# Two first dst and two sums per block: the halves of a graph kernel's edge blocks added up apart

## The chip, the cores and the metric

One core of a Trainium2 chip runs the whole kernel in one launch. The metric is the device time of one execution in microseconds, the median of several runs. Four compute engines matter: TensorE (PE, whose weight loads the profile lists as PEld), VectorE (DVE), ScalarE (ACT) and GpSimd (POOL). SyncE (SP) issues DMAs.

## The reference

There are V = 12500 nodes with 64 features and E = 400000 edges, sorted by `dst`. `src` is uniform; `dst` is drawn as `12500 * uniform ** 2`, so the density of edges falls from the low nodes to the high ones.

```python
h = x @ W_lin + b_lin
agg1 = segment_sum(h[src], dst) / deg
h = tanh(agg1 @ W1_agg + h @ W1_root + b1)
agg2 = segment_sum(h[src], dst) / deg
x = layernorm(x + tanh(agg2 @ W2_agg + h @ W2_root + b2))
hn = x @ Wn.T + bn
w = ssp(edge_feats @ We1.T + be1)          # ssp = softplus - log 2, per edge
w = ssp(w @ We2.T + be2)
agg = segment_sum(hn[src] * w, dst)
x = layernorm(x + ssp(agg @ Wc.T + bc) @ Wp.T + bp)
```

So there are three sums of gathered rows over the edges: two of 16-feature rows (stages e1 and e2) and one of 64-feature rows, each multiplied by an edge's gate (stage e3).

## The kernel before, in words

The edges are cut into NB = 125 blocks of 3200, each laid out as 128 partitions of SLOTS = 25 slots: partition p holds edges 25p to 25p + 24 of its block. Slots 0 to 12 are half 0 and slots 13 to 24 are half 1 (`HALVES`). With this layout each half has edges from the whole block.

A block is added up by matmul. For a window of WIN = 128 nodes, VectorE builds a one-hot matrix per slot (`make_hot`: is this edge's dst the w-th node of the window?), and TensorE multiplies each slot's gathered rows by it, 25 matmuls into one PSUM tile `sums` (`add_up`, L717 and L974). VectorE then adds `sums` onto the accumulator `acc` at the window's first node (L805 and L1153). That is one visit. A block needs as many visits as windows that its dst span, counted from its own first dst. The setup block computes for each block its first and last dst, hence the number of visits, a running count of them (`visits`), and subtracts the block's first dst from `dst_f`. `windows` reads from `visits` the registers of a block: since, to, and for VectorE the first dst. The visits are a loop from since to to.

Stages e1 and e2 run `pick_phase`. 14 of a block's slots are gathered from a table in memory by GpSimd, one indirect DMA a slot (L645), into one of four buffers. The other 11 slots are picked on chip: ScalarE makes one-hot keys (L666, L670), TensorE multiplies them with the table (L699, 88 matmuls of 400 columns a block), in four groups of 3, 3, 3 and 2 slots, and VectorE reduces the result (`take`, L758). After the fourth take VectorE splits the picked rows into bf16 parts (`parts`). TensorE's order is: pick group 0 of the next block, add up this block, pick groups 1, 2 and 3 of the next. `pick` waits for ScalarE's keys and for the take of the group before the last. VectorE's order is: read the registers, build half 0's hot of the first window, take(3), parts, then in each visit build half 1, build half 0 of the following window (also when there is none), wait for TensorE, and add; then `block_used` (L806), which frees the gather buffer for GpSimd four blocks on, and the takes 0 to 2 of the next block.

Stage e3 runs `gate_phase` with two gather buffers, 23 gathered slots (L922) and 2 picked ones (L957, 28 matmuls a slot). An edge MLP computes the gates: `first_layer` (L940) and `second_layer` (L947) on TensorE, logs and exponentials on ScalarE, the rest on VectorE. VectorE's `add_up` waits for a block's gathers, multiplies them by the gates (L1128), computes `second_values` of the next block (L1082), builds half 0's hot (L1116), takes the picked slot and runs the visits. TensorE's order is pick, second layer, pick, first layer of the block after next, add up.

All orders are written out by hand; there is no planner. SP loads keys, indices and edge features ahead.

Of the kernel before, what the change touches and what calls it, by code (L numbers as in the profile page):

```python
# [21 lines left out]
P = 128  # L22
# [63 lines left out]
def gnn_kernel(nc, x, xw, src, src_sel, src_gate, dst_all, edge_t, W_linT, b_lin, W1_agg, W1_root, b1, W2_parts, W2_diag, WnT, bn, We1T, be1,  # L86
               We2T, be2, WcT, bc, WpT, bp, out):
    ctx = ExitStack()
    with ctx:
# [40 lines left out]
        base_diag = sb("base_diag", [NB, NB])  # L130
# [33 lines left out]
        ext_t = sb("ext_t", [NB, 2])  # L164
        ext_i = sb("ext_i", [NB, 1], I32)
        win_lo = sb("win_lo", [NB, 1])
        win_hi = sb("win_hi", [NB, 1])
        win_n = sb("win_n", [NB, 1])
        win_row = sb("win_row", [1, NB])
        visits = sb("visits", [1, 3 * NB], I32)  # L170
# [104 lines left out]
        dst_ext = tiles.enter_context(nc.sbuf_tensor("dst_ext", [P, 2, NB], F32))  # L275
# [22 lines left out]
        with nc.Block() as block:  # L298
# [86 lines left out]
            def _(pe):  # L385
# [26 lines left out]
                for k in range(2):  # L412
# [3 lines left out]
                pe.matmul(bank[5][0:1, 0:NB], win_n[:, :], upto[0:NB, 0:NB], start=True, stop=True)  # L416
                pe.matmul(bank[5][0:1, NB:2 * NB], win_n[:, :], ident[0:NB, 0:NB], start=True, stop=True)
                pe.matmul(bank[5][0:1, 2 * NB:3 * NB], win_lo[:, :], ident[0:NB, 0:NB], start=True, stop=True)
                pe.matmul(bank[7][:, 0:NB], ones_all[:, :], base_diag[:, :], start=True,
# [6 lines left out]
            def _(dve):  # L426
# [33 lines left out]
                for c in range(2):  # L460
                    if c == 1:
# [3 lines left out]
                        dve.tensor_reduce(dst_ext[:, 0, :], dst_f[:, :, :], AX.X, ALU.min)  # L465
                        dve.tensor_reduce(dst_ext[:, 1, :], dst_f[:, :, :], AX.X, ALU.max).then_inc(small, 1)
# [66 lines left out]
                dve.tensor_reduce(ext_t[:, 0:1], bank[5][0:NB, 0:P], AX.X, ALU.min)  # L533
                dve.tensor_reduce(ext_t[:, 1:2], bank[5][0:NB, P:2 * P], AX.X, ALU.max)
                dve.drain()
                dve.tensor_copy(win_lo[:, :], ext_t[:, 0:1])
                dve.tensor_tensor(win_hi[:, :], ext_t[:, 1:2], ext_t[:, 0:1], ALU.subtract)
                dve.drain()
                dve.tensor_copy(ext_i[:, :], win_hi[:, :])
                dve.tensor_scalar(base_diag[:, :], ident[0:NB, 0:NB], win_lo[:, :], None, ALU.mult)  # L540
# [7 lines left out]
                dve.tensor_tensor(dst_f[:, :, :], dst_f[:, :, :],  # L548
# [22 lines left out]
        def pick_phase(tag, table, full, buf, hots, tiles):  # L571
# [34 lines left out]
            with nc.Block() as block:  # L606
# [133 lines left out]
                def _(dve):  # L740
# [46 lines left out]
                    def body(n, g, u):  # L787
# [903 lines left out]
```

## Time and profile before

| | |
|---|---|
| Median of 3 runs | 8763.72 us (8760.71 to 8766.48) |
| Profiled execution, first to last instruction | 8760.1 us |
| PE / PEld busy | 7637.1 us (87%) / 6905.6 us (79%) |
| DVE busy | 5505.1 us (63%) |
| ACT busy | 5860.1 us (67%) |
| POOL busy | 6259.5 us (71%) |
| Mean granted TensorE clock | 0.951 of full speed |

For the profiled execution the profile gives the span alone; the median of the runs is 3.6 us above it. e1 runs from about 96 to 2424 us, e2 to 4827 us, e3 from about 4960 to 8702 us; between them are short stages over the nodes.

A line of the profile's groups reads: source line, engine, operation, output<-inputs, shapes, count, then busy time and mean of one in ns, then idle time of the engine just before them and what ended it. Register reads and semaphore instructions are not counted as busy; an idle time that they end is put down to "issue". The engine name with a q is that engine's sequencer.

### The profile page before, as it was taken

How to read it: one execution, taken by the hardware profiler on the slowest of the kernel's cores; microseconds unless marked ns; L12 is line 12 of the kernel's file. 1: busy time of each engine (PE TensorE's matmuls, PEld its weight loads, DVE VectorE, ACT ScalarE, POOL GpSimd, SP SyncE). 2: the span in 40 equal slices, each digit the busy share in tenths (PEclk: the TensorE clock that was granted, in tenths of full speed). 3: DMA queues.
4: the chain of work that ended last, by engine and by line, in shares of the span. 5: the costliest groups of instructions: out<-in, count | busy, mean ns of one | idle time of the engine just before them, and what ended most of it. 6: DMA issues, size and time to landing. Idle time of an engine off the chain costs nothing. (4 is left out here: it accounts for less than half of the span.)

```text
span 8760.1 us, 165117 instructions
## 1 busy us (share of the span) xinstructions
PE 7637.1 (87%) x51516; PEld 6905.6 (79%) x51517; DVE 5505.1 (63%) x7447; ACT 5860.1 (67%) x10176; POOL 6259.5 (71%) x6471
## 2 busy tenths in 40 slices
PE   7999999999989999999999777777777777888887
PEld 6999999888889999998888666666666666776775
DVE  5655656666645555556666666666666666777777
ACT  5777777666657777776666566666666666666665
POOL 5777777766557777777664477777777777777776
PEclk9999999999989999999999798988988889999999
DMA  2111112111111111111111222222222222222222
GB/s 75 35 34 35 35 34 35 31 30 28 25 40 34 35 34 35 34 34 31 31 30 23 75 56 59 55 57 57 55 58 56 55 59 55 55 59 56 55 56 59
DMA packets 341135, 392.62 MB, mean 45 GB/s; under 512 B 165119, under 2 KB 240563, under 8 KB 340564
## 3 DMA queue, kind: packets, MB, share of 16 engines
q0 software_dynamic: 204000, 151.96, 12.1%
q1 hardware_dynamic: 136750, 239.87, 8.1%
q8 instruction: 32, 0.52, 0.0%
q14 instruction: 31, 0.25, 0.0%
q10 hardware_dynamic: 322, 0.03, 0.0%
HBM read 375.47 MB, written 15.92 MB: 45 GB/s over the span
## 5 line engine op out<-in xcount | busy, mean ns | idle before, releaser
L699 PE MATMUL banks<-split_sb,e_low_hot 128*128 128x400 f32 x22000 | 4092.6, 346 | 45.6 <-DVE split_sb L752 45.6
L699 PEld LDWEIGHTS banks<-split_sb,e_low_hot 128*128 128x128 f32 x22000 | 4015.6, 189 | 74.1 <-DVE split_sb L752 46.1
L922 POOL DMA_INDIRECT big<-hn_table,src_i x2875 | 2857.0, 994 | 883.7 <-issue 870.7
L645 POOL DMA_INDIRECT big<-p_table,src_i x1750 | 1655.8, 946 | 695.2 <-issue 528.7
L758 DVE TENSOR_REDUCE picked<-banks 128x48 f32<-128x1200 f32 x1000 | 1300.1, 1300 | 1352.1 <-PE banks L699 1351.1
L670 ACT ACTIVATE e_low_hot<-e_key_off 128x1536 fp32r<-128x1536 f16 x1000 | 1381.1, 1381 | 1130.6 <-PE banks L699 1112.7
L645 POOL DMA_INDIRECT big<-h_table,src_i x1750 | 1674.9, 957 | 612.5 <-issue 529.6
L666 ACT ACTIVATE e_key_off<-e_key_in,node_off 128x384 f16<-128x384 f16 (+1 forms) x4000 | 2028.4, 577 | 125.5 <-DMA e_key_in<-sel_dram 41.4
L957 PE MATMUL banks<-hn_split,e_low_hot 128*128 128x448 f32 x7000 | 1500.1, 370 | 75.5 <-issue 70.1
L957 PEld LDWEIGHTS banks<-hn_split,e_low_hot 128*128 128x128 f32 x7000 | 1298.0, 188 | 217.1 <-issue 96.6
L781 DVE TENSOR_TENSOR hot<-e_dst_pair,banks 128x1536 bf16<-128x1536 bf16 (+1 forms) x934 | 931.1, 997 | 69.9 <-issue 0.6
L1006 ACT ACTIVATE e_wide<-e_wide 128x512 f32<-128x512 f32 x500 | 268.9, 538 | 1041.3 <-DVE e_wide L1082 1041.3
L940 PE MATMUL banks<-e_wide,we 128*128 128x512 f32 x1000 | 553.5, 715 | 441.9 <-DVE e_wide L1082 431.7
L1116 DVE SCALAR_TENSOR_TENSOR hot<-dst_f,win_base,banks 128x1664 f32<-128x1664 f32 (+1 forms) x467 | 872.6, 1894 | 64.7 <-issue 50.3
L974 PEld LDWEIGHTS banks<-hot,big 128*64 128x64 f32 x8550 | 512.1, 144 | 397.0 <-DVE hot L1116 330.2
L974 PE MATMUL banks<-hot,big 128*64 128x128 f32 x8550 | 595.0, 289 | 262.7 <-DVE hot L1116 231.4
L940 PEld LDWEIGHTS banks<-e_wide,we 128*128 128x128 f32 x1000 | 254.0, 266 | 697.9 <-DVE e_wide L1082 521.8
L1128 DVE SCALAR_TENSOR_TENSOR big<-e_wide,big 128x1600 f32<-128x1600 f32 x125 | 228.3, 1826 | 891.8 <-DMA big<-hn_table,src_i 889.1
L1035 ACT ACTIVATE e_low_hot<-e_key_in,node_off 128x128 fp32r<-128x128 f16 x1750 | 535.7, 387 | 178.0 <-PE banks L957 178.0
L1012 ACT ACTIVATE e_wide<-e_wide 128x512 f32<-128x512 f32 x1000 | 550.3, 550 | 68.1
L1010 ACT ACTIVATE e_wide<-e_wide 128x512 f32<-128x512 f32 x1000 | 550.4, 550 | 67.7
L717 PE MATMUL banks<-hot,big 128*64 128x128 bf16 x8550 | 376.0, 226 | 209.1 <-DVE acc L805 114.0
(216 smaller groups left out, 4491.7 us busy)
## 6 DMA issues: line engine op xcount, KB each, us to landing
e_wide<-in_edge_t SPq DMA_DIRECT2D x125, 832.0 KB
e_key_in<-sel_dram SPq DMA_DIRECT2D x250, 343.8 KB
big<-hn_table,src_i POOLq DMA_INDIRECT x2875
big<-p_table,src_i POOLq DMA_INDIRECT x1750
big<-h_table,src_i POOLq DMA_INDIRECT x1750
e_key_in<-gate_dram SPq DMA_DIRECT2D x125, 64.0 KB
src_i<-in_src SPq DMA_DIRECT2D x375, 12.5 KB, 1.7
e_key_in<-sel_dram SPq DMA_DIRECT2D x250, 8.2 KB
```

The source lines that it names most:

```text
L645: pool.indirect_dma_start(buf[u][:, j, 0:ROW0], None, table, bass.IndirectOffsetOnAxis(ap=src_i[u][:, j:j + 1], axis=0),).then_inc(gathere ...
L666: act.activation(off[:, h, :], key_in[u][:, es], ACT.Abs, bias=node_off[:, h:h + 1])
L670: act.activation(low_hot[gr][:, :, :], off, ACT.Relu, bias=1.0, scale=-1.0).then_inc(low_made, 1)
L699: last = pe.matmul(o, low_hot[gr][:, h, e], split_sb[:, part, h * HI1:(h + 1) * HI1, :], start=(h == 0 and part == 0), stop=(h == HI2 - 1 ...
L758: dve.tensor_reduce(picked[:, AT[gr]:AT[gr] + SIZE[gr], :], found, AX.X, ALU.max).then_inc(pick_taken, 1)
L781: dve.tensor_tensor(hots[h].rearrange("p j (w t) -> p j w t", t=2), dst_pair[:, a:b, :].unsqueeze(2).to_broadcast([P, b - a, WIN // 2, 2]) ...
L922: pool.indirect_dma_start(buf[u][:, j, 0:F], None, table, bass.IndirectOffsetOnAxis(ap=src_i[u][:, j:j + 1], axis=0),).then_inc(gathered[u ...
L940: pe.matmul(pZ[q][:, 0:w], we1_2[:, :], xT_e[u][:, cs], start=True, stop=True).then_inc(z1_psum, 1)
L957: last = pe.matmul(bank[c][:, 0:GHALF * F], low_hot[s][:, h, :], hn_split[:, part, h * GHIGH + c * GHALF:h * GHIGH + (c + 1) * GHALF, :], ...
L974: last = pe.matmul(sums[c:c + F, 0:WIN], buf[u][:, j, 0:F], hots[h][:, j - a, :], start=(j < 2), stop=(j >= SLOTS - 2))
L1010: act.activation(o, o, ACT.Exp, scale=-1.0)
L1116: dve.scalar_tensor_tensor(hots[h], d.unsqueeze(2).to_broadcast([P, b - a, WIN]), win_base[:, bass.ds(window, 1)], iota_ps.unsqueeze(1).to ...
```

## The change

The host lays the edges out anew: the first 1664 edges of a block go to half 0 (partition p holds 13p to 13p + 12), the other 1536 to half 1 (12 a partition). `src`, `dst` and the edge features follow. Each half now has its own first dst, its own number of visits and running count, its own sums (columns 0 to 127 and 128 to 255 of a PSUM bank) and its own semaphore `acc_added`. A half's visits are a loop of their own on TensorE and on VectorE. No hot is built ahead of its visit.

```diff
-        def windows(eng, n, with_first):
-            since = eng.value_load(visits[0:1, bass.ds(n, 1)], ...)
-            to = eng.value_load(visits[0:1, bass.ds(n + NB, 1)], ...)
+        def windows(eng, n, h, with_first):
+            since = eng.value_load(visits[0:1, bass.ds(n + h * NB, 1)], ...)
+            to = eng.value_load(visits[0:1, bass.ds(n + (2 + h) * NB, 1)], ...)
             if not with_first:
                 return since, to, None
-            first = eng.value_load(visits[0:1, bass.ds(n + 2 * NB, 1)], ...)
+            first = eng.value_load(visits[0:1, bass.ds(n + (4 + h) * NB, 1)], ...)
...
             # pick_phase, TensorE
-                    def add_up(n, g, u):
-                        since, to, _ = windows(pe, n, False)
-                        pe.wait_ge(gathered[u], 16 * took * (g + 1))
-                        pe.wait_ge(msgs_made, n + 1)
+                    def add_up(h, n, g, u):
+                        a, b = HALVES[h]
+                        since, to, _ = windows(pe, n, h, False)
+                        if h == 0:
+                            pe.wait_ge(gathered[u], 16 * took * (g + 1))
+                        else:
+                            pe.wait_ge(msgs_made, n + 1)
                         pe.sem_inc(waited, 1)
                         with pe.Fori(since, to) as visit:
-                            pe.wait_ge(acc_added, visit + 1)
-                            for h, (a, b) in enumerate(HALVES):
-                                pe.wait_ge(hot_made[h], visit + 1 + (n if h == 0 else 0))
-                                for j in range(a, b):
-                                    ...
-                                last.then_inc(hot_used[h], 1)
+                            pe.wait_ge(acc_added[h], visit + 1)
+                            pe.wait_ge(hot_made[h], visit + 1)
+                            for j in range(a, b):
+                                ...
+                            last.then_inc(hot_used[h], 1)
                     def body(n, g, u):
                         if inside(n + 1):
                             pick(0, n + 1)
-                        add_up(n, g, u)
+                        add_up(0, n, g, u)
                         if inside(n + 1):
                             pick(1, n + 1)
+                        add_up(1, n, g, u)
+                        if inside(n + 1):
                             pick(2, n + 1)
                             pick(3, n + 1)
...
             # pick_phase, VectorE
-                    def body(n, g, u):
-                        since, to, first = windows(dve, n, True)
-                        make_hot(0, n, 0, since + 1)
-                        take(3, n)
-                        parts(u)
+                    def half(h, n, since, to, first):
                         with dve.Fori(since, to) as visit:
                             ...
-                            make_hot(1, n, window, visit + 1)
-                            make_hot(0, n, window + 1, visit + 2)
-                            dve.wait_ge(hot_used[1], visit + 2)
-                            dve.wait_ge(acc_added, visit + 1)
+                            make_hot(h, n, window, visit + 1)
+                            dve.wait_ge(hot_used[h], visit + 2)
                             a_w = acc[:, bass.ds(start, WIN)]
-                            dve.tensor_tensor(a_w, a_w, sums[:, 0:WIN], ALU.add).then_inc(acc_added, 1)
+                            dve.tensor_tensor(a_w, a_w, sums[h], ALU.add).then_inc(acc_added[h], 1)
+                    def body(n, g, u):
+                        since, to, first = windows(dve, n, 0, True)
+                        take(3, n)
+                        parts(u)
+                        half(0, n, since, to, first)
+                        if inside(n + 1):
+                            take(0, n + 1)
+                        since, to, first = windows(dve, n, 1, True)
+                        half(1, n, since, to, first)
                         dve.sem_inc(block_used, 1)
                         if inside(n + 1):
-                            for gr in range(3):
-                                take(gr, n + 1)
+                            take(1, n + 1)
+                            take(2, n + 1)
...
             # gate_phase, TensorE (add_up changed as above; its drain and block_used after half 1)
                     def body(n, g, u):
                         pick(n + 1, 0)
                         second_layer(n + 1)
                         pick(n + 1, 1)
+                        add_up(0, n, u)
                         if not isinstance(n, int) or n + 2 < NB:
                             first_layer(n + 2, turn_of(g, u) + 1, u % 2)
-                        add_up(n, g, u)
+                        add_up(1, n, u)
...
             # gate_phase, VectorE (half as above)
-                        make_hot(0, n, 0, since + 1)
+                        half(0, n, since, to, first)
                         if values_ahead:
                             take(n + 1, 1, (u + 1) % 2)
-                        with dve.Fori(since, to) as visit:
-                            ...
+                        since, to, first = windows(dve, n, 1, True)
+                        half(1, n, since, to, first)
...
             # host
+    def by_slot(a):
+        blocks = np.asarray(a).reshape(NB, EB, -1)
+        parts = [blocks[:, P * j:P * k].reshape(NB, P, k - j, -1) for j, k in HALVES]
+        return np.concatenate(parts, axis=2)
```

In the setup block the minima and maxima of dst are taken for each half (four reductions over halves instead of two over all slots), four rows are transposed instead of two, six row matmuls instead of three give the counts and first dst, the matmul with `base_diag` is twice as wide, `dst_f` is lowered in two subtractions, and `visits` is filled by four copies and two subtractions instead of two and one.

## Rows read from the trace of the kernel before

**Rows 1.** Windows by stretch: engines' busy us (instructions), then clock, DMA share, GB/s.

```profile
100.00:1458.00 1358.00, 1347.39 (x8822) 1308.11 (x8822) 803.86 (x1167) 1064.56 (x1561) 1027.01 (x1087) 1.00 0.19 35
1520.00:2424.00 904.00, 815.37 (x6029) 778.26 (x6028) 564.36 (x879) 580.53 (x851) 564.95 (x598) 0.98 0.15 28
...
5000.00:7320.00 2320.00, 1807.15 (x10976) 1449.60 (x10976) 1451.75 (x1724) 1460.81 (x3130) 1774.46 (x1790) 0.90 0.23 57
```

**Rows 2.** block_used by stretch: count, ns min/median/max, first to last start.

```profile
L806 DVEq EVENT_SEMAPHORE  x78: 21/21/21, 121.1 to 1458.8; - x78
L806 DVEq EVENT_SEMAPHORE  x44: 21/21/21, 1536.9 to 2424.1; - x44
L806 DVEq EVENT_SEMAPHORE  x78: 21/21/21, 2524.5 to 3864.8; - x78
L806 DVEq EVENT_SEMAPHORE  x45: 21/21/21, 3926.0 to 4827.1; - x45
```

**Rows 3.** The page's group of hot builds in e1 and e2: count, busy, mean.

```profile
L781 DVE TENSOR_TENSOR hot<-e_dst_pair,banks 128x1536 bf16<-128x1536 bf16 (+1 forms) x934 | 931.1, 997 | 69.9 <-issue 0.6
```

**Rows 4.** GpSimd's gathers, single-visit stretches of e1 and e2, columns of rows 2.

```profile
L645 POOL DMA_INDIRECT big<-p_table,src_i x1120: 940/944/1114, 149.9 to 1549.4; - x187
L645 POOL DMA_INDIRECT big<-h_table,src_i x1071: 951/955/1123, 2549.8 to 3899.7; - x179
```

**Rows 5.** Timeline, e1, one single-visit block: start, duration, engine, [idle before].

```profile
1006.45 16.27 PE L699 MATMUL banks<-split_sb,e_low_hot 128*128 128x400 f32 x88
1015.47 1.41 DVE L758 TENSOR_REDUCE picked<-banks 128x48 f32<-128x1200 f32 x1 [2.96 <-PE banks L699]
1018.26 0.24 DVE L778 TENSOR_SCALAR e_dst_pair<-dst_f,win_base 128x26 bf16 x1 [1.39 <-issue]
1019.52 0.98 DVE L758 TENSOR_REDUCE picked<-banks 128x32 f32<-128x800 f32 x1
1022.59 0.95 DVE L781 TENSOR_TENSOR hot<-e_dst_pair,banks 128x1536 bf16<-128x1536 bf16 x1
1022.64 0.42 PEld L717 LDWEIGHTS banks<-hot,big 128*64 128x64 bf16 x13 [0.27 <-issue]
1023.60 0.53 PE L717 MATMUL banks<-hot,big 128*64 128x128 bf16 x12 [0.38 <-DVE hot L781]
```

**Rows 6.** L717 single-visit, then two-visit: idle before, PE plus weight load, us, times.

```profile
  DVE hot L781: 27.5, 76
...
  DVE hot L781: 133.3, 170
  DVE acc L805: 53.7, 44
```

**Rows 7.** Timeline: the last block of e1, nothing queued before it.

```profile
2418.94 1.74 PE L717 MATMUL banks<-hot,big 128*64 128x128 bf16 x25 [3.46 <-issue]
```

**Rows 8.** e3's gating, single-visit then two-visit stretch, with its idle time.

```profile
L1128 DVE SCALAR_TENSOR_TENSOR big<-e_wide,big x76: 1824/1826/1827, 5045.2 to 7281.8; 128x1600 f32<-128x1600 f32 x76
  DMA big<-hn_table,src_i: 674.5, 76
...
L1128 DVE SCALAR_TENSOR_TENSOR big<-e_wide,big x45: 1824/1826/1827, 7341.5 to 8658.9; 128x1600 f32<-128x1600 f32 x45
  DMA big<-hn_table,src_i: 194.5, 45
```

**Rows 9.** Timeline, e3, one single-visit block.

```profile
5999.26 1.83 DVE L1128 SCALAR_TENSOR_TENSOR big<-e_wide,big 128x1600 f32<-128x1600 f32 x1 [9.06 <-DMA big<-hn_table,src_i]
6000.31 1.60 POOL L922 DMA_INDIRECT big<-hn_table,src_i  x1 [0.30 <-issue]
6011.63 0.29 DVE L1153 TENSOR_TENSOR acc<-acc,banks 128x128 f32 x1
```

**Rows 10.** Timeline of the setup block.

```profile
73.15 0.27 DVE L551 COPY win_row<-banks 1x125 f32<-1x125 f32 x1
```

More of the change, by code:

```diff
@@ L591, in pick_phase @@
             msgs_made = sem(f"{tag}_msgs_made")
-            sums = bank[7]
+            sums = [bank[7][:, h * WIN:(h + 1) * WIN] for h in range(2)]
             iota_ps = bank[6][:, 0:WIN // 2]
@@ L794, in body @@
                                 visit - since, 0, NW - 1,
-                                skip_runtime_bounds_check_because="a block's dst span NW windows at most")
+                                skip_runtime_bounds_check_because="a half's dst span NW windows at most")
                             start = nc.s_assert_within(
@@ L838, in gate_phase @@
             hot_used = [sem(f"{tag}_hot_used{h}") for h in range(2)]
-            acc_added = sem(f"{tag}_acc_added")
-            sums = bank[7]
+            acc_added = [sem(f"{tag}_acc_added{h}") for h in range(2)]
+            sums = [bank[7][:, h * WIN:(h + 1) * WIN] for h in range(2)]
             iota_ps = bank[6][:, 0:WIN]
@@ L1120, in make_hot, with half @@
                             ALU.subtract, ALU.is_equal).then_inc(hot_made[h], 1)
+                    def half(h, n, since, to, first):
+                        with dve.Fori(since, to) as visit:
+                            window = nc.s_assert_within(
+                                visit - since, 0, NW - 1,
+                                skip_runtime_bounds_check_because="a half's dst span NW windows at most")
+                            start = nc.s_assert_within(
+                                first + window * WIN, 0, V - 1,
+                                skip_runtime_bounds_check_because="a visit starts at or before a dst")
+                            make_hot(h, n, window, visit + 1)
+                            dve.wait_ge(hot_used[h], visit + 2)
+                            a_w = acc[:, bass.ds(start, WIN)]
+                            dve.tensor_tensor(a_w, a_w, sums[h], ALU.add).then_inc(acc_added[h], 1)
                     def add_up(n, g, u, values_ahead=True):
-                        since, to, first = windows(dve, n, True)
+                        since, to, first = windows(dve, n, 0, True)
                         dve.wait_ge(gathered[u], 16 * took * (g + 1))
@@ L1136, in add_up @@
                         dve.drain()
-                        make_hot(0, n, 0, since + 1)
+                        half(0, n, since, to, first)
                         if values_ahead:
                             take(n + 1, 1, (u + 1) % 2)
-                        with dve.Fori(since, to) as visit:
-                            window = nc.s_assert_within(
-                                visit - since, 0, NW - 1,
-                                skip_runtime_bounds_check_because="a block's dst span NW windows at most")
-                            start = nc.s_assert_within(
-                                first + window * WIN, 0, V - 1,
-                                skip_runtime_bounds_check_because="a visit starts at or before a dst")
-                            make_hot(1, n, window, visit + 1)
-                            make_hot(0, n, window + 1, visit + 2)
-                            dve.wait_ge(hot_used[1], visit + 2)
-                            dve.wait_ge(acc_added, visit + 1)
-                            a_w = acc[:, bass.ds(start, WIN)]
-                            dve.tensor_tensor(a_w, a_w, sums[:, 0:WIN], ALU.add).then_inc(acc_added, 1)
+                        since, to, first = windows(dve, n, 1, True)
+                        half(1, n, since, to, first)
                     def body(n, g, u):
```

122 lines of the change are left out of this document (69 added, 53 removed).

## The prediction

> **What bounds the kernel now.** I read the busy shares by stretch first [rows 1]. The run has three long stages, e1, e2 and e3. In e1's first stretch TensorE is busy 1347 of 1358 us at clock 1.00; GpSimd has 1027 us of gathers in the same time, and its gaps are short ones between gathers. So TensorE is at its limit there, with GpSimd close by. In e1's second stretch TensorE's share falls to 90% (815 of 904). In e3 it is 78% at clock 0.90: TensorE isn't the limit there.
>
> Then the signal with which VectorE ends a block [rows 2]. In e1's first stretch 77 intervals take 1458.8 - 121.1 us: 17.37 us a block. In the second it is (2424.1 - 1536.9) / 43 = 20.63, and in e2's second (4827.1 - 3926.0) / 44 = 20.48. The reference explains the step: dst is 12500 u^2, sorted, so block n of 125 spans about 0.8 (2n + 1) nodes. That is under 128 up to n = 79 and at most 199 after it: one visit, then two. The 934 hot builds of the two stages [rows 3] bear it out: each stage makes one for every block and two for every visit, 467 = 125 + 2 x 171. So there are 171 visits a stage, and 46 blocks have two.
>
> GpSimd sets a floor under both [rows 4]: 1399.5 us over 1119 gathers is 1.251 each, 14 a block, 17.51 us; in e2 (3899.7 - 2549.8) / 1070 makes 17.66.
>
> For e3 I read the gating operation, which starts when a block's gathers land [rows 8]. It recurs every (7281.8 - 5045.2) / 75 = 29.82 us with one visit and every 29.94 us with two, and VectorE sits idle for the gathers before every one of them: 8.9 us a block, then 4.3. One gather more or less is what e3 feels; a visit isn't.
>
> **Part 1: fewer visits in e1 and e2.** A half spans about half of a block's nodes: 0.8 (2n + 1) x 0.52, at most 104, so every half has one visit. Add-up matmuls fall from 171 x 25 to 125 x 25 a stage, hot builds from 467 to 250, and the two-visit blocks go. What one block costs afterwards I work out on the single-visit block of the timeline [rows 5]. From the first pick matmul (1006.45) to the add-up (1022.64) is 16.19 us for 88 matmuls, 0.183 each with one entry into an add-up; the entry shows 0.27 idle, 0.09 more than the usual spacing. The add-up itself is 0.55 for 13 (1022.64 to 1023.60 less the 0.38 wait is 0.58) and 0.52 for 12.
>
> **Part 2: the second entry.** TensorE now loads its two registers twice a block. Behind 24 queued pick matmuls that costs again 0.1 us net; with nothing queued it shows 3.46 us of idle time [rows 7], which is the upper bound. I take 0.1, since pick group 1 has as many matmuls as group 0.
>
> **Part 3: hot builds no longer made ahead.** Before, half 0's build ran before VectorE's take of group 3, and the next window's build was made whether wanted or not. Now half 0 is built after take(3) and the split into parts. TensorE's pick(0) starts 24 x 0.183 + 0.09 before 1022.64, at 1018.16, and the result of group 3 reaches VectorE at about 1018.4. Take(3) to the end of a build is 1019.52 to 1023.54 in the rows, 4.02; with 13 slots 4.1. So hot 0 is ready at 1022.5, 0.1 us before TensorE wants it: no wait, without slack. VectorE then waits for the add-up (1023.4), adds (0.28), takes group 0 (1.41), and reads three registers for half 1. The rows give that read: take dispatched 1015.47, next operation 1018.26, 2.8 us, of which 1.4 lies under the take. Starting the take at 1023.95, the build starts at 1026.7 and ends at 1027.95. TensorE, with pick(1) from 1023.2, is ready at 1027.7. That is a wait of 0.3 us. Behind it are picks 2 and 3; their takes have over 1 us to spare.
>
> One block: 16.19 + 0.55 + 0.52 + 0.1 + 0.3 = 17.65 us. Bounds: 17.35 without the wait, which GpSimd's 17.51 and 17.66 then replace; upward, an unhidden 3.46 twice a block is the far end, but the near rows are the waits for hot builds and sums in two-visit blocks [rows 6]: 133.3 + 53.7 us over 44 blocks, double counted for TensorE and its weight load, so some 2 us for four half add-ups, 0.5 each. With 0.5 at both halves it is 18.35.
>
> **Sum of e1 and e2.** From first to last signal is 2303.0 us in e1 and 2302.6 in e2 [rows 2]; after, 124 x 17.65 = 2188.6. The first signal comes later, 10.6 us instead of 6.1 us after its picks, +4.5. So -109.9 and -109.5: -219.
>
> **Part 4: e3.** Block 78's successors lose 0.12 us each: 45 x 0.12 = -5. The tail has one visit less: -2. The chain from gating to the last sum is now 12.7 us in a single-visit block (5999.26 to 6011.92) [rows 9]; after, the speculative build (about 1.9) goes, but there are two round trips to TensorE, two sums and a second register read: 16 to 18 us. That takes 4 to 5 of the 8.9 us idle, and about nothing where it is 4.3, as two visits go there. GpSimd waits for block_used two blocks back and has over 10 us left. ScalarE's first logs follow first_layer, which moves behind add_up(0): its first result comes about 2 us later, when ScalarE is just done with the second logs. Cover gone, each us of chain beyond the idle time costs 125 us.
>
> GpSimd's gather under the gating operation takes 1.60 us instead of 0.95 [rows 9], while e1's and e2's gathers, with hot builds beside them all the time, have a median within 4 ns of their shortest [rows 4]. So 217 hot builds fewer give GpSimd nothing in e3; the operation that it contends with stays.
>
> **Part 5: setup.** Two transposes, three row matmuls, four small copies and a subtraction more, and one more diagonal, each like the 0.27 of the win_row copy [rows 10], mostly in series: +2.5 us (0 to 5).
>
> **Sum.** 8760.1 - 219 - 7 + 2.5 = 8536.6 for the profiled execution; the runs' median lies 3.6 us above its span. Forecast 8540.
>
> **A rule weighed.** The rows have the three-register read at 2.8 us from the take's dispatch, and TensorE's exposed part at 0.27 us [rows 5]. The Trainium skill, DMA: Bandwidth & Descriptors (the table with the `tensor_load` floor), puts one such load at about 600 ns or more. By that figure alone TensorE's two loads are 1.2 us at each entry, and exposed they would make this change worth, by an estimate from that page, 250 x 1.1 = 275 us less than forecast, a loss. The trace disagrees for the exposed part behind a full queue, and agrees for VectorE, roughly.
>
> **Rivals.**
> A. No waits: hots arrive in time, and the floor is GpSimd. e1 at 17.5, e2 at 17.55 (its gathers start ahead of TensorE by two blocks): 248 x 0.12 = 30 us less, 8510. For it: TensorE's single-visit rate of 17.37 still holds waits. Against: half 1's chain on VectorE is 0.3 late by my own count.
> B. VectorE's chain becomes the bound. Each build, sum and register read is in series with TensorE, 0.6 us a block more: 248 x 0.6 = 149, 8690. For it: no slack at hot 0, and 20.6 us in two-visit blocks where VectorE and TensorE alternate. Against: there the second visit has no pick between, here each add-up has one.
> C. Slower: the register loads at the added entry are not hidden. From 0.9 us more a block (219 / 248) the gain is gone; at the rows' idle 3.46 less 0.27, every other block, it is 1.6 x 248 = 397, less 225: 8940. For it [rows 7]; against it [rows 5], with 24 matmuls ahead of the entry as now.
> D. Slower: e3 becomes chain-bound. Its clock is 0.90 on average already [rows 1], TensorE works in bursts after VectorE, and now in more of them; if the period passes 31.6 us (29.8 + 219 / 125) the gain is gone; at 32 it is 8540 + 270 = 8810. The Trainium skill, TensorE: Matmul & The Clock Gate (Part 1), says that activity releases the clock and idleness halves it. Against: the idle time of 8.9 us has to be used up first.
> E. The edit does not lower the visits (first dst per half far from the half's range): the numbers of dst above exclude it but for chance.
>
> **How the numbers follow.** Forecast 8540 (17.5 to 17.9 a block: 8510 to 8605) 0.58; A 0.17; B 0.17; C 0.03; D 0.04; E 0.01. What can be told from no change is 0.2%, 18 us. A, the forecast and nearly all of B are faster by more: 0.92. C, D and a B that goes further give slower 0.06; same 0.02. Range 8490 to 8650: the forecast's own, A, and B's nearer half.
>
> **What would show it.** L717 matmuls 6250, L781 500, L1116 250. Every block of e1 and e2 in 17.5 to 17.8 us, with no step at block 79. TensorE waits for hot builds at the second half, none at the first. The gating operation of e3 still every 29.8 us, with idle time before it of 4 to 5 us in all blocks. Wrong if a block of e1 takes over 18, if "issue" before L717 grows over 0.5 us each, or if that idle time in e3 is gone.

## The result and the profile after

The changed kernel takes 8527.36 us (median of four runs, 8525.02 to 8529.87) against 8764.24: a ratio of 0.9727, 95% interval 0.9713 to 0.9741. Run again beside the last experiments it took 8531.62 against 8762.99, 0.9736 (0.972 to 0.9752). The forecast was 8540, the range 8490 to 8650.

One thing has to be known to read the experiments: eight of the twelve (the first two runs of the old layout, and everything from "Both halves behind one pick group" to "e3: first_layer ahead; registers up front") ran while the kernel before itself took 12488 to 12524 us (medians), so their times stand only against one another, and what they say of the undisturbed kernel comes from the last blocks of a stage, which show no disturbance; the other four ran beside 8761 to 8763 us. None of the eight came out at the time, or in its loops at the time of a block, that was expected of it.

The page of the changed kernel has, in its first part, busy us (share of the span) and instructions, and in its fifth the groups (count, busy, mean ns, idle before):

```profile
PE 7506.0 (88%) x46924; PEld 6812.9 (80%) x46925; DVE 4727.1 (55%) x6607; ACT 5879.0 (69%) x10176; POOL 6267.9 (74%) x6471
...
L991 PE MATMUL banks<-hot,big 128*64 128x128 f32 x6250 | 563.3, 342 | 768.6 <-DVE hot L1137 768.6
L1137 DVE SCALAR_TENSOR_TENSOR hot<-dst_f,win_base,banks 128x1664 f32<-128x1664 f32 x250 | 470.3, 1881 | 270.2 <-issue 270.2
L794 DVE TENSOR_TENSOR hot<-e_dst_pair,banks 128x1664 bf16<-128x1664 bf16 x500 | 494.1, 988 | 44.4 <-issue 11.8
```

Hot builds in e1 and e2 are 500 in place of 934 [rows 3], and 250 in e3. The signal that ends a block, e1 then e2 (count, ns, first to last us), answers to [rows 2]:

```profile
L823 DVEq EVENT_SEMAPHORE  x125: 21/21/21, 129.1 to 2303.1; - x125
L823 DVEq EVENT_SEMAPHORE  x125: 21/21/21, 2409.1 to 4580.8; - x125
```

That is 2174.0 / 124 = 17.53 us a block and 2171.7 / 124 = 17.51, all the way through; the step at block 79 is gone. Windows in the middle of e1, e2 and e3 (columns of [rows 1]):

```profile
1000.00:2000.00 1000.00, 996.77 (x6455) 952.36 (x6454) 547.40 (x798) 777.87 (x1141) 756.81 (x799) 1.00 0.19 34
3500.00:4500.00 1000.00, 996.27 (x6450) 953.07 (x6449) 549.63 (x799) 778.52 (x1143) 758.58 (x793) 1.00 0.19 34
5500.00:7500.00 2000.00, 1559.40 (x9379) 1313.24 (x9380) 1133.35 (x1471) 1259.95 (x2676) 1531.19 (x1539) 0.89 0.23 56
```

TensorE is busy 99.7% of the time in e1 and e2, 90% before in e1's two-visit stretch. In e3 it is busy as before, at clock 0.89.

Where the 233.0 us between the two profiled spans (8760.1 and 8527.1) went, from the signals and the gatings of both traces: up to e1's first signal +8.1; e1 -129.0; from there to e2's first signal +5.6; e2 -130.9; to e3's first gating +1.3; e3 (first to last gating, 3688.3 and 3697.2) +8.9; tail +3.1.

One block of e1, cut to the two entries of the add-up (timeline; start, duration, engine, [idle before]); it answers to [rows 5]:

```profile
1507.46 1.02 DVE L794 TENSOR_TENSOR hot<-e_dst_pair,banks 128x1664 bf16<-128x1664 bf16 x1
1508.64 0.58 PE L728 MATMUL banks<-hot,big 128*64 128x128 bf16 x13
1509.15 4.64 PE L710 MATMUL banks<-split_sb,e_low_hot 128*128 128x400 f32 x24
1509.44 0.29 DVE L812 TENSOR_TENSOR acc<-acc,banks 128x128 f32 x1 [0.96 <-PE banks L728]
1509.72 1.41 DVE L771 TENSOR_REDUCE picked<-banks 128x48 f32<-128x1200 f32 x1
1512.42 0.24 DVE L791 TENSOR_SCALAR e_dst_pair<-dst_f,win_base 128x24 bf16 x1 [1.29 <-issue]
1512.73 0.95 DVE L794 TENSOR_TENSOR hot<-e_dst_pair,banks 128x1536 bf16<-128x1536 bf16 x1
1513.80 0.39 PEld L728 LDWEIGHTS banks<-hot,big 128*64 128x64 bf16 x12 [0.35 <-issue]
```

Hot 1 is built at 1513.69; TensorE's pick group 1 ends at 1513.79. The profile names no wait for a hot here. Over 1000 to 2000 us TensorE's weight load has 115 entries with idle time, all put down to "issue":

```profile
  issue: 36.8, 115
```

That is 0.32 us each, against 0.26 in the kernel before, where half 0's hot was ready 3.0 to 3.5 us early. There is a wait in it. TensorE's sequencer waits for the build's semaphore in one instruction of its own, at L725; in this block it is

```profile
L725 PEldq EVENT_SEMAPHORE  x1: 51/51/51, 1513.7 to 1513.7; - x1
```

and in the trace it starts 0.039 us after the build ends. It does so, to 0.001 us, in all 456 entries from 200 to 2200 and from 2500 to 4500 us, while the time since the last pick matmul varies: TensorE's sequencer is released by VectorE's build every time. At half 1 the weight load follows 0.115 us after the build's end in every block, with a mean idle time of 0.34 us in e1 and 0.36 in e2; at half 0 it is 0.30 and 0.26. So hot 1 comes about 0.1 us late in every block, and hot 0 at most 0.05.

In e3 the gating operation (count, ns, first and last us; then its idle time by cause) answers to [rows 8], and the timeline of one block to [rows 9]:

```profile
L1163 DVE SCALAR_TENSOR_TENSOR big<-e_wide,big x125: 1824/1826/1879, 4755.4 to 8452.6; 128x1600 f32<-128x1600 f32 x125
...
  DMA big<-hn_table,src_i: 285.0, 102
  issue: 31.6, 23
```

```profile
6004.09 1.82 DVE L1163 SCALAR_TENSOR_TENSOR big<-e_wide,big 128x1600 f32<-128x1600 f32 x1 [1.75 <-DMA big<-hn_table,src_i]
6014.33 1.08 DVE L1129 TENSOR_REDUCE big<-e_masked 128x64 f32<-128x896 f32 x1
6017.12 1.82 DVE L1137 SCALAR_TENSOR_TENSOR hot<-dst_f,win_base,banks 128x1536 f32<-128x1536 f32 x1 [1.70 <-issue]
6019.08 1.53 PE L991 MATMUL banks<-hot,big 128*64 128x128 f32 x24 [3.62 <-DVE hot L1137]
6020.83 0.29 DVE L1155 TENSOR_TENSOR acc<-acc,banks 128x128 f32 x1 [1.90 <-PE banks L991]
```

The period is still 3697.2 / 124 = 29.82 us. The chain from gating to last sum has become 6021.12 - 6004.09 = 17.0 us (12.7 before), and the idle time before a gating 316.6 / 125 = 2.5 us (8.9 and 4.3 before). At e3's start GpSimd now waits for its first buffer (0.6 us there before):

```profile
4773.74 1.01 POOL L940 DMA_INDIRECT big<-hn_table,src_i  x1 [5.63 <-PEq L995]
```

### The profile page after: what moved, and what is told of

Same layout as the page of the kernel before. It is cut to its first block and busy times, and to the rows that moved or that the text cites. A ratio compares the mean times of both kernels' runs of the same rounds, so it can differ in the third digit from the quotient of the medians.

```text
span 8527.1 us, 164066 instructions
## 1 busy us (share of the span) xinstructions
PE 7506.0 (88%) x46924; PEld 6812.9 (80%) x46925; DVE 4727.1 (55%) x6607; ACT 5879.0 (69%) x10176; POOL 6267.9 (74%) x6471
## 5 line engine op out<-in xcount | busy, mean ns | idle before, releaser
L710 PE MATMUL banks<-split_sb,e_low_hot 128*128 128x400 f32 x22000 | 4136.2, 346 | 46.8 <-DVE split_sb L765 25.2
L940 POOL DMA_INDIRECT big<-hn_table,src_i x2875 | 2860.6, 995 | 890.0 <-issue 859.0
L975 PE MATMUL banks<-hn_split,e_low_hot 128*128 128x448 f32 x7000 | 1594.5, 387 | 76.3 <-issue 69.8
L975 PEld LDWEIGHTS banks<-hn_split,e_low_hot 128*128 128x128 f32 x7000 | 1387.5, 201 | 236.0 <-issue 108.5
L991 PE MATMUL banks<-hot,big 128*64 128x128 f32 x6250 | 563.3, 342 | 768.6 <-DVE hot L1137 768.6
L1137 DVE SCALAR_TENSOR_TENSOR hot<-dst_f,win_base,banks 128x1664 f32<-128x1664 f32 x250 | 470.3, 1881 | 270.2 <-issue 270.2
L794 DVE TENSOR_TENSOR hot<-e_dst_pair,banks 128x1664 bf16<-128x1664 bf16 x500 | 494.1, 988 | 44.4 <-issue 11.8
L1126 DVE TENSOR_TENSOR e_masked<-banks,e_high 128x896 f32<-128x896 f32 x250 | 272.9, 1092 | 346.9 <-PE banks L975 326.3
L958 PE MATMUL banks<-e_wide,we 128*128 128x512 f32 x1000 | 426.8, 573 | 11.1 <-DMA e_wide<-in_edge_t 11.1
L1155 DVE TENSOR_TENSOR acc<-acc,banks 128x128 f32 x250 | 72.2, 289 | 656.3 <-PE banks L991 656.3
L1163 DVE SCALAR_TENSOR_TENSOR big<-e_wide,big 128x1600 f32<-128x1600 f32 x125 | 228.3, 1827 | 316.6 <-DMA big<-hn_table,src_i 285.0
```

What stands on the lines that cost most here:

```text
L710: last = pe.matmul(o, low_hot[gr][:, h, e], split_sb[:, part, h * HI1:(h + 1) * HI1, :], start=(h == 0 and part == 0), stop=(h == HI2 - 1 ...
L794: dve.tensor_tensor(hots[h].rearrange("p j (w t) -> p j w t", t=2), dst_pair[:, a:b, :].unsqueeze(2).to_broadcast([P, b - a, WIN // 2, 2]) ...
L940: pool.indirect_dma_start(buf[u][:, j, 0:F], None, table, bass.IndirectOffsetOnAxis(ap=src_i[u][:, j:j + 1], axis=0),).then_inc(gathered[u ...
L975: last = pe.matmul(bank[c][:, 0:GHALF * F], low_hot[s][:, h, :], hn_split[:, part, h * GHIGH + c * GHALF:h * GHIGH + (c + 1) * GHALF, :], ...
L991: last = pe.matmul(sums[h][c:c + F, :], buf[u][:, j, 0:F], hots[h][:, j - a, :], start=(j < a + 2), stop=(j >= b - 2))
```

## The experiments

The theory: the gain is the visits that the layout saves; the second entry costs TensorE next to nothing, because a pick group stands between the halves, and VectorE reaches hot 1 just in time; e3 stays bound by GpSimd. Rivals: the splitting of the sums alone gives the gain; VectorE or TensorE has reserve; e3's chain is about to take over.

### Old layout

```
-        blocks = np.asarray(a).reshape(NB, EB, -1)
-        parts = [blocks[:, P * j:P * k].reshape(NB, P, k - j, -1) for j, k in HALVES]
-        return np.concatenate(parts, axis=2)
+        return np.asarray(a).reshape(NB, P, SLOTS, -1)
```

> The changed kernel's program with the edges laid out as before: each half has edges of the whole block, so blocks from 79 on have two visits in each half. Theory 1 (the gain is the second visits that fall away; the new order by itself costs a little): the first 79 blocks of e1 keep 17.53 us, the later ones have two extra round trips between VectorE and TensorE of some 2.3 us each behind no pick work, 22 us or more, against 20.6 before; in e3 the chain of two-visit blocks grows by some 5 us and passes the 2.5 us of idle time that is left. Slower than before, 8850 to 9050 us. Rival (the gain is the order: no hot built ahead, sums apart behind two pick groups): the time stays under 8650 us, and the later blocks of e1 take at most 19 us.

> The kernel of e1_old_layout again, on a chip that runs the kernel before near 8764 us: the changed kernel's program, but each half has edges of the whole block, so two visits in each half from block 79 on. Theory 1 (the gain is the second visits that fall away, the new order by itself costs a little): 17.5 us for the early blocks of e1, 21 to 23 us for the later ones, in e3 the two-visit blocks pass their idle time; slower than before, 8850 to 9050 us. Rival (the gain is the order): under 8650 us, at most 19 us for the later blocks.

> The edges of a block lie in the slots as in the kernel before, so a half's destinations span as much as the whole block's: 171 visits a half and stage in place of 125; the program is otherwise the changed one. Theory A (the gain comes from the layout alone, through the visits it saves): the blocks up to 77 stay at 17.5 us in the first two stages, those from 80 on become 24 to 25 us (TensorE's last three blocks of this edit showed 23.4 to 25.9), more than the 20.2 us of the kernel before, and the whole lands at or above the kernel before, by up to 2 x 46 x 4 = 370 us in the first two stages and something more in the third. Theory B (the gain comes from splitting the sums apart and putting a pick group between): at or under 17.5 + 3 = 20.5 us in the late blocks, the whole within 1% of the kernel before or under it.

Measured: 1.1257 (1.1161 to 1.1354) and 1.1282 (1.1199 to 1.1365) of the kernel before in the first two, and 9657.55 us, 1.1021 (1.1003 to 1.104), in the third. The signals of e1 in its trace, single-visit and two-visit stretch:

```profile
L823 DVEq EVENT_SEMAPHORE  x78: 21/21/21, 127.6 to 1478.3; - x78
L823 DVEq EVENT_SEMAPHORE  x44: 21/21/21, 1572.3 to 2673.6; - x44
```

(1478.3 - 127.6) / 77 = 17.54 us, as in the changed kernel; (2673.6 - 1572.3) / 43 = 25.61, 5.0 more than the 20.63 of the kernel before. The idle time ahead of TensorE's add-up from 1718 us on:

```profile
  issue: 218.3, 150
  DVE hot L794: 187.2, 77
```

And e3's gating in the two-visit stretch:

```profile
L1163 DVE SCALAR_TENSOR_TENSOR big<-e_wide,big x37: 1824/1826/1886, 8188.8 to 9574.9; 128x1600 f32<-128x1600 f32 x37
...
  issue: 47.1, 36
```

The period there is 1386.1 / 36 = 38.5 us, and no gating waits for a gather any more. So the fewer visits carry the gain: the same program with the old layout is 1126 us slower than with the new one (e1 +372, e2 +363, e3 +390, from the stages of both traces), and 10% slower than the kernel before. The split sums make a second visit dearer (no hot is built ahead, and no pick stands between the two visits of a half): +8.1 us a block where it was +3.3. Theory A stands; its sizes were too small: 25.6 us a block where 24 to 25 was expected, 475 us lost against the kernel before in e1 and e2 where 370 was the most, and in e3 not "something more" but about 400. The new layout in the old program was not run; there a block's windows are counted from the block's own first dst, so its visits would stay 171 a stage.

### Both halves behind one pick group

```
-                        if inside(n + 1):
-                            pick(1, n + 1)
                         add_up(1, n, g, u)
                         if inside(n + 1):
+                            pick(1, n + 1)
```

On VectorE, half 1's registers are read up front, and take(0) stands behind half 1.

> New layout, one visit a half, but in e1 and e2 both halves are added up at one place, behind pick group 0 (on VectorE half 1 follows half 0 at once, with its registers read ahead of take 3). Theory 1: the second pick group is what hides VectorE's way from the sum of half 0 over the build of hot 1 (0.24 + 0.95) to TensorE; without it TensorE idles 1.5 to 2.5 us a block, so a block of e1 takes 19 to 20 us and the kernel 8900 to 9150 us, slower than before although visits fell. Rival (fewer visits are all there is to it): 17.4 to 17.7 us a block, 8500 to 8550.

> The kernel of e2_together again: new layout, but both halves added up at one place behind pick group 0 in e1 and e2. Theory 1 (the second pick group hides VectorE's way from sum 0 over the build of hot 1 to TensorE): 19 to 20 us a block, 8900 to 9150 us. Rival (fewer visits are all there is to it): 17.4 to 17.7 us a block, 8500 to 8550.

Measured: 1.0743 (1.0679 to 1.0806) and 1.0761 (1.0696 to 1.0826). The last three blocks of e1 took 22.9, 21.5 and 23.2 us in the first, 17.8, 17.0 and 17.5 in the changed kernel. That is more than either theory has; the edit stands undisturbed under "One edit in each stage".

### VectorE reads more, TensorE reads more

Two register reads more ahead of half 1, on VectorE in the first, on TensorE in the second:

```
+                        windows(dve, n, 1, False)
```

```
+                        if h == 1:
+                            windows(pe, n, h, False)
```

> In e1 and e2 VectorE reads two registers more ahead of half 1 (some 1.4 us more in its sequencer). In the trace of the changed kernel the build of hot 1 ends 0.1 us before TensorE is ready for it. If that is so (theory: VectorE is just in time, no slack), TensorE waits 1.2 to 1.4 us at each half 1: 18.7 to 18.9 us a block, 8820 to 8880 us in all. Rival (VectorE has slack, TensorE alone sets 17.5): no change, 8527.

> In e1 and e2 TensorE reads two registers more ahead of add_up(1), some 1.2 to 1.4 us more in its sequencer. Theory A (the reads lie under the 24 queued pick matmuls, the 0.27 us idle is a fixed price of the entry): no change, 8527 within 20 us. Theory B (the 0.27 us idle is what sticks out of the reads, so each further read shows in full): 18.7 to 18.9 us a block, 8820 to 8880.

Measured: 1.0358 (1.0306 to 1.041) and 1.0313 (1.0262 to 1.0364). In the second the last three blocks of e1 took 17.77, 16.99 and 17.45 us, to the hundredth what they take in the changed kernel: TensorE's reads are hidden. They run ahead under the 24 queued matmuls, and TensorE's sequencer has time: in the block shown above its two reads end at 1511.85 and it reaches the loop at 1512.19, then it waits for hot 1 until 1513.73. Those 1.5 us are just what two more reads take (0.75 us from one read to the next), so a third is not shown to be free. In the first they took 18.39, 18.16 and 19.06: VectorE's reads are not hidden. The 0.1 us of lead that the expectation starts from is the way of the semaphore to TensorE, as shown above; VectorE is the one waited for already.

### e3: first_layer ahead; registers up front

The third adds, to the VectorE edit of e1 and e2, that first_layer stands ahead of add_up(0) in e3; the fourth, to the TensorE edit, that VectorE reads half 1's registers together with half 0's:

```
                         pick(n + 1, 1)
-                        add_up(0, n, u)
                         if not isinstance(n, int) or n + 2 < NB:
                             first_layer(n + 2, turn_of(g, u) + 1, u % 2)
+                        add_up(0, n, u)
```

```
                         since, to, first = windows(dve, n, 0, True)
+                        since1, to1, first1 = windows(dve, n, 1, True)
```

> Two edits in separate stages, read apart in the trace. In e1 and e2 VectorE reads two registers more ahead of half 1 (1.4 us more in its sequencer). Theory (VectorE just in time at hot 1, 0.1 us ahead in the trace): 18.7 to 18.9 us a block, e1 and e2 together 300 to 340 us longer than in the changed kernel. Rival (slack): 17.5. In e3 first_layer stands ahead of add_up(0), as before the change. Theory (GpSimd's gathers bound e3; the order on TensorE only moves idle time about): the gating operation still every 29.8 us, from first to last within 5 us of 3697. Rival (e3 lost 13 us to TensorE's order and clock): some 10 us less.

> Two edits in separate stages. In e1 and e2 TensorE reads two registers more ahead of add_up(1) (1.2 to 1.4 us more in its sequencer). Theory A (the reads lie under the queued pick matmuls): 17.5 us a block. Theory B (the 0.27 us idle at an entry is what sticks out, and each further read shows in full): 18.7 to 18.9 us. In e3 VectorE reads half 1's registers together with half 0's, before it waits for the gathers. Theory (the chain from gating to the last sum is 17 us, 1.7 of them this read): the chain is 15.3 us, VectorE's idle time before gating grows from 2.5 to 4 us, and the time of e3 does not change but for 1 to 2 us of GpSimd's wait of 5.6 us at its third block.

Measured: 1.0538 (1.0478 to 1.0598) and 1.0444 (1.0385 to 1.0502). e3, first to last gating, took 5574.4 us with first_layer ahead (5346.8 without) and 5511.8 with the reads up front (5376.8 without). Neither helps there. But e3 is not bound by GpSimd in that condition (43 us a block), so these two say little of the undisturbed stage.

### The changed kernel again, and a longer chain in e3

```
+                        windows(dve, n, 1, True)
+                        windows(dve, n, 1, True)
                         since, to, first = windows(dve, n, 1, True)
                         half(1, n, since, to, first)
```

> The changed kernel itself, unaltered, on whatever chip the other variants meet. On a chip where the kernel before takes about 8764 us, every theory expects 0.973 of it, blocks of 17.5 us in the first two stages and 29.8 us in the third. On a chip like the two on which the variants ran (the kernel before 12490 to 12524 us), theory A, that TensorE's added register read costs nothing and the stalls there come per instruction issued, expects this kernel level with the variant that reads TensorE's registers twice: 1.03 of the kernel before, first two stages at 28.2 us a block and 17.4 us in their last three blocks. Theory B, that the added read is paid where instructions come slowly, expects at least 1 us a block less than the variant, so at or under 1.01.

> Two more sets of three register reads on VectorE, ahead of half 1 in the third stage alone: its chain from a gating to the next one becomes longer by 4 to 5 us a block. Theory A (the third stage ends with GpSimd, and VectorE's idle time ahead of a gating, 2.5 us in the mean, is the whole of the chain's room): the stage goes from 29.8 to 31.3 to 32.5 us a block, 190 to 330 us in all. Theory B (idle time elsewhere in the chain takes it up as well, since TensorE's picks are early): under 50 us in all. The first two stages stay as they are. Where the chip stalls TensorE at every instruction, the third stage is bound by that and by this chain already, and each block takes the whole 4 to 5 us.

Measured: 0.9736 (0.972 to 0.9752) for the changed kernel; e1, e2 and e3 at 17.53, 17.52 and 29.81 us a block. The comparison that was to tell its two theories apart needs the 12500 us condition, which this run didn't meet; it stays open. With the longer chain 8843.97 us, 1.0092 (1.0076 to 1.0109). e1 and e2 are unchanged. The gating's rows:

```profile
L1163 DVE SCALAR_TENSOR_TENSOR big<-e_wide,big x125: 1824/1826/1889, 4754.2 to 8763.1; 128x1600 f32<-128x1600 f32 x125
...
  issue: 162.3, 124
```

4008.9 / 124 = 32.33 us a block, 2.5 more, 312 us in all, and none of them waits for a gather. The idle time before hot builds in e3 is, in this kernel:

```profile
  issue: 731.5, 250
```

The changed kernel has 270.2 in the page row of L1137 above, so six reads are (731.5 - 270.2) / 125 = 3.69 us, 0.61 each. Of 3.7 us added (4 to 5 were expected), 2.5 reached the period: e3's chain has 1.2 us in hand. That is the idle time for gathers of 2.5 less the 1.3 of "issue" (162.3 / 124) that remain even when the chain is the bound. The range of theory A held.

### One edit in each stage

e1 with both halves behind one pick group (and half 1's registers read up front), e2 with VectorE's two extra reads, e3 with the registers up front; each edit is as shown above, save that e1 reads half 1's registers behind `parts` and not ahead of take(3); they stand under `if tag == "e1"` or `"e2"`.

> One edit in each stage, all read apart from one another by stage. First stage: both halves are added up behind pick group 0, with no pick group between them, and the next block's first take stands behind both. If the pick group between the halves is what hides building hot 1 and its round trip, a block goes from 17.5 to 20.8 to 23 us (what the last three blocks of this edit showed before); if TensorE were bound by its own work alone, it stays at 17.5. Second stage: two register reads more on VectorE ahead of half 1. If VectorE arrives just in time for hot 1, a block goes from 17.5 to 18.1 to 18.7 us; if it has more than 1.4 us in hand, it stays. Third stage: VectorE reads half 1's three registers up front with half 0's. If the stage is bound by GpSimd's gathers, its blocks stay at 29.8 us and only the start-up wait of 5.6 us becomes smaller, 0 to 10 us in all; if the reads were on the path that sets the end, it loses 1 to 2 us a block, 120 to 250 us.

Measured: 9486.61 us, 1.0826 (1.0808 to 1.0844). The signals of e1 and e2:

```profile
L829 DVEq EVENT_SEMAPHORE  x125: 21/21/21, 129.2 to 3090.7; - x125
L829 DVEq EVENT_SEMAPHORE  x125: 21/21/21, 3197.1 to 5524.0; - x125
```

e1: 2961.5 / 124 = 23.88 us a block, 6.35 more, and over the 20.8 to 23 expected. A block of it in the timeline:

```profile
1509.07 0.24 DVE L793 TENSOR_SCALAR e_dst_pair<-dst_f,win_base 128x26 bf16 x1 [2.34 <-issue]
1510.55 0.55 PE L728 MATMUL banks<-hot,big 128*64 128x128 bf16 x13 [2.15 <-DVE hot L796]
1513.39 0.85 PE L728 MATMUL banks<-hot,big 128*64 128x128 bf16 x12 [2.29 <-DVE hot L796]
1514.17 17.05 PE L710 MATMUL banks<-split_sb,e_low_hot 128*128 128x400 f32 x82
```

The first wait of 2.15 us is the edit's own: three more reads stand ahead of hot 0. The second, 2.29, is what the pick group between the halves hides: VectorE's sum and its building of hot 1. TensorE's own register reads end about 1 us before hot 1 is built. Behind them TensorE runs slower: the add-up of 12 takes 0.85 in place of 0.53, and 82 pick matmuls 0.208 us each in place of 0.186 (59 in 10.96 in the changed kernel). The window of that kernel has the granted clock at 0.86, where it was 1.00:

```profile
1000.00:2000.00 1000.00, 814.94 (x4728) 788.13 (x4727) 402.88 (x588) 569.75 (x836) 554.97 (x586) 0.86 0.14 25
```

So two gaps of 2.2 us cost 6.35 together, some 1.9 of it (82 x 0.022) by the slower picks after them.

e2: 2326.9 / 124 = 18.77, 1.25 more (18.1 to 18.7 expected). TensorE's idle time ahead of the add-ups over 3500 to 4500 us:

```profile
  issue: 99.8, 106
  DVE hot L796: 69.9, 53
```

The profile names one wait for a hot a block, 1.3 us ahead of the matmul: the two reads (1.2 by the 0.61 above) go straight through. VectorE has nothing in hand. The same 53 waits stand a second time in the first line, as 1.62 us of "issue" ahead of the weight load: the profile puts a wait for a hot down to "issue" there, as it does in the changed kernel.

e3: 3711.7 us against 3697.2; the idle time before a gating is twice as long, so the chain is shorter, and the period is not:

```profile
L1172 DVE SCALAR_TENSOR_TENSOR big<-e_wide,big x125: 1824/1826/1868, 5699.7 to 9411.4; 128x1600 f32<-128x1600 f32 x125
...
  DMA big<-hn_table,src_i: 607.0, 120
```

GpSimd bounds it. The start-up wait (5.65 us) did not shrink, and the stage became 14.5 us longer, by the expectation 0 to 10 shorter. GpSimd's busy time in e3 is 17.0 us more (2877.6 against 2860.6, summed over 2875 gathers): more of them run above 1 us (374 against 253). The trace says which: 250 of them start while VectorE runs the `e_wide` operation of L1118 (L1110 in the changed kernel, 129 there) and run 31 us longer for it; those that start under the gating run 14 us shorter. So the earlier chain moved VectorE's work onto more gathers.

## Why the prediction was right, and where it was not

**Part 1, fewer visits: right.** 125 visits a half and stage, the trace holds 6250 add-up matmuls of e1 and e2, no step. The old layout in the same program shows that the gain goes with them.

**Part 2, the second entry: right.** 0.1 us net was forecast. From the last pick matmul to the add-up's first takes 0.28 us in the kernel before; here it is 0.39 (e1) and 0.41 (e2) at half 1, 0.33 and 0.28 at half 0. Less these 0.16 and 0.13 us of waiting for hots, a block takes 17.4 us, close to the 17.35 of the sum without its wait. Doubling TensorE's reads changes none of the three blocks of e1 that can be compared. Rival C falls. Its price was misread as well: the 3.46 us of [rows 7] are no cost of reads with nothing queued. In that block TensorE's two reads are over at 2413.3, under its last pick matmuls, and then its sequencer waits 5.18 us for `parts`, which VectorE ends at 2418.50:

```profile
L708 PEldq EVENT_SEMAPHORE  x1: 5176/5176/5176, 2413.4 to 2413.4; - x1
```

**Part 3, hot 1 late by 0.3 us: right in kind, wrong in size.** I let VectorE's take of group 0 begin 1.31 us after TensorE begins half 0 (1023.95 - 1022.64); it begins at 1509.72 - 1508.64 = 1.08, because the sum follows the add-up's end sooner than I took it. So the build ends 5.04 us after TensorE's start instead of 5.31. TensorE, by the forecast ready 5.06 after it, starts at 5.16, 0.115 after the build's end. A lateness of 0.3 is one of 0.1. The block is 17.52 instead of 17.65, and 248 x 0.13 = 32 us is the gap in e1 and e2 (-259.9 between signals, where 2 x 114.2 = 228.4 was forecast). Rival A's number, 17.5, was met, and neither of its reasons: TensorE waits at half 1 in every block, and GpSimd is no floor, since it ends a block's gathers 24 us ahead of TensorE all through e1 and, in e2, 2.2 us ahead still at the last block. That VectorE's chain is the near danger (rival B) was right: 1.2 us more on it costs 1.25 a block.

**The first signals:** +4.5 each forecast, +8.1 (with the setup, 3.4) and +5.6 measured.

**Part 4, e3: -7 forecast, +13.3 measured** (+1.3, +8.9, +3.1). The step that failed is that the stage's start was left out. The first five intervals between gatings take 134.3 us before and 141.3 after, +7.0, as GpSimd waits 5.6 us for the longer chain where it waited 0.6. The other 119 intervals take 3554.1 and 3555.9: +1.8 where 45 x 0.12 was to give -5. In the trace of the second run of the changed kernel the two parts are 144.6 and 3552.4, so the start's part is +7 to +10 and that of the rest +2 to -2. The chain itself was at the upper end or over it (16 to 18 forecast): 17.0 us in one block, and 18.6 (6034.04 to 6052.64) in the next, where the granted clock is 0.57 from 6037 to 6045 us and the 26 matmuls of half 0 take 3.22 us, not 1.71. So 2.5 us are idle, not 4 to 5, and only 1.2 of them can be used, as the longer chain showed. Rival D was nearer than its chance of 0.04 said.

**Part 5, setup: right,** +3.4 to the first gather (78.1 to 81.4 us) for +2.5.

The sum gave 8536.6 for the profiled execution, which took 8527.1: 32 us too little gained in e1 and e2, 20 too little lost in e3, 2 in setup and first signals. That the forecast of 8540 came within 13 us owes something to luck, as the errors of Parts 3 and 4 have opposite signs. The median lies 0.3 us above the span, not 3.6.

**The rule weighed.** The Trainium skill, DMA: Bandwidth & Descriptors, has one register load at about 600 ns or more. The runs agree as to VectorE, with 0.61 each over six; on TensorE they follow one another at 0.75, and behind 24 queued matmuls two more cost nothing.

## What to carry to other kernels

Count how often data make a loop run before tuning its body: laying 46 blocks' edges so that each half fits one window was worth more than all that the added entry, reads and round trips cost. When one unit of work is split in two, put independent work of the other engine between the halves, and check the second engine's chain to a tenth of a microsecond, since both sides were balanced here. An idle time that the profile calls "issue" can hold a wait: if the same few nanoseconds lie between the end of another engine's instruction and the waiting one in every block, the first releases the second. A stage that "doesn't care" still has a chain with a room; measure the room, it was 1.2 us where its idle time showed 2.5.

## What the runs showed of the hardware

**GpSimd is next.** In e2 the last gather of block 0 ends at 2381.0 and TensorE begins to add that block up at 2403.0: 22.0 us ahead. At block 124 it is 4572.4 and 4574.6: 2.2 us. 14 gathers take 17.67 us, TensorE's block 17.51, so the lead that GpSimd has at the stage's start is used up just at its end, and a faster TensorE should gain little more in e2; no run tried it.

**VectorE's gating holds up GpSimd's gathers.** In e3 a gather takes 0.95 us, and one that starts while the gating operation runs ends 2.65 us after that operation's start (the median of 125 in the kernel before, nearly all within 2.64 and 2.68), wherever in it the gather began: in the changed kernel one that began 0.06 us into it takes 2.60 us, one 1.24 us into it 1.43. That end is 0.8 us after the operation's own, so GpSimd seems to be held until the gating is over.

**A disturbed condition.** While the kernel before took 12500 us, TensorE's pick matmuls stood apart in the loops. Timeline of the variant with TensorE's extra reads, e1:

```profile
2000.07 0.49 PE L710 MATMUL banks<-split_sb,e_low_hot 128*128 128x400 f32 x1 [1.78 <-issue]
2001.47 0.49 PE L710 MATMUL banks<-split_sb,e_low_hot 128*128 128x400 f32 x1 [0.91 <-issue]
2003.55 0.49 PE L710 MATMUL banks<-split_sb,e_low_hot 128*128 128x400 f32 x1 [1.59 <-issue]
```

Gaps of 0.9 to 1.8 us wait for nothing that the profile shows. They take some 10 us a block (28.2 against 17.5) inside the loop, and are absent from the last three blocks of a stage, which lie in the straight code behind it. One and the same chip ran in this condition and later without it. What causes it stays open; that instructions came to TensorE late is only argued. In it the variant whose reads cost nothing in those last blocks took 1.03 of the kernel before; the changed kernel itself was never run there.
